# A decoder of four layers on one core: cross attention's inputs loaded by the stage ahead, a self attention with its norm and a longer lead, experts with three buffers

## The reference, cut to what matters

```python
def sublayer(x):              # layer norm without a weight, residual
    return x + f((x - mean(x)) / sqrt(var(x) + 1e-5))
# layer 0: self attention (16 heads of 64, weights of 1024 columns), mixing with the context, coupled twist
# layer 1: gated recurrence, cross attention (16 heads of 8), experts (32, 6 chosen)
# layer 2: linear attention, cross attention, experts (8, 2 chosen)
# layer 3: rotary attention (two), cross attention, experts (32, 2 chosen, at most 70 tokens each) with 16 shared adapters
```

## Time and profile before

| | us |
|---|---|
| median of 3 runs | 4221.11 (4218.85 to 4239.77) |
| the profiled execution | 4235.5 |
| its span | 4233.7 |
| PE busy | 3635.9 (86%) |
| DVE busy | 2555.3 (60%) |
| ACT busy | 2097.0 (50%) |
| POOL busy | 1549.6 (37%) |
| the 16 DMA engines, mean | 110 GB/s |

### The profile page before, as it was taken

One profiled execution on the slowest core, in us unless ns is written; L12 is line 12 of the kernel. 1 busy time (PEld: TensorE's weight loads), 2 busy tenths in 40 slices (PEclk: granted clock), 3 DMA queues, 4 the chain that ended last, 5 costly groups with the idle time before them and its releaser, 6 DMA issues. The chain is left out here.

```text
span 4233.7 us, 113113 instructions
## 1 busy us (share of the span) xinstructions
PE 3635.9 (86%) x48174; PEld 2505.2 (59%) x48174; DVE 2555.3 (60%) x4447; ACT 2097.0 (50%) x2832; POOL 1549.6 (37%) x1827
## 2 busy tenths in 40 slices
PE   7976459999997888799999988988899999972798
PEld 5654237777775446477777764434477777751565
DVE  4522568877774445578777753346688777746443
ACT  3344437666664232267666652344476666650010
POOL 1100037667661000267667620013466766610000
PEclk9998779999998899899999998989999999985897
DMA  4062045655651430456655621100465566510674
GB/s 147 2 253 102 2 108 148 151 145 148 157 140 37 98 85 3 96 137 152 152 142 150 157 50 55 54 8 9 105 150 147 141 156 150 143 42 0 159 184 123
DMA packets 203247, 464.39 MB, mean 110 GB/s; under 512 B 87486, under 2 KB 94398, under 8 KB 202590
## 3 DMA queue, kind: packets, MB, share of 16 engines
q1 hardware_dynamic: 200622, 455.30, 41.3%
q10 hardware_dynamic: 2160, 2.29, 0.2%
HBM read 212.72 MB, written 1.72 MB: 51 GB/s over the span
## 5 line engine op out<-in xcount | busy, mean ns | idle before, releaser
L1435 DVE TENSOR_REDUCE x_bank_top<-ps 112x1 f32<-112x500 f32 x2304 | 1418.7, 671 | 472.0 <-PE ps L1151 465.6
L1287 ACT ACTIVATE x_probs_t<-ps 128x1344 f32<-128x1344 f32 x768 | 991.2, 1291 | 215.0 <-PE ps L1168 210.4
L1168 PEld LDWEIGHTS ps<-x_queries,x_keys 128*128 128x128 bf16 x9216 | 488.7, 98 | 333.5 <-issue 152.9
L1151 PE MATMUL ps<-x_keys,x_queries 96*112 96x500 bf16 x2304 | 633.7, 381 | 25.0 <-DMA x_keys<-x_key_part 15.6
L1168 PE MATMUL ps<-x_queries,x_keys 128*128 128x112 bf16 x9216 | 585.4, 213 | 41.2 <-ACT x_probs_t L1287 36.6
L1181 PE MATMUL ps<-x_probs_t,x_values 128*32 128x112 f32 x18432 | 492.2, 263 | 5.3 <-ACT x_probs_t L1287 4.1
L1181 PEld LDWEIGHTS ps<-x_probs_t,x_values 128*32 128x32 f32 x18432 | 445.0, 111 | 70.1 <-issue 65.2
L1368 POOL TENSOR_TENSOR x_key_part<-x_key_whole,x_nothing 128x500 bf16<-128x500 f32 x270 | 336.8, 1247 | 259.3 <-ACT x_key_whole L1272 259.3
L1372 POOL TENSOR_TENSOR x_key_part<-x_key_left,x_nothing 128x500 bf16<-128x500 f32 x270 | 340.3, 1260 | 21.2
L1139 PE MATMUL ps<-x_wv,x_ctx_t 128*128 128x128 f32 (+1 forms) x2304 | 329.9, 287 | 9.8 <-issue 9.8
L1151 PEld LDWEIGHTS ps<-x_keys,x_queries 96*112 96x112 bf16 x2304 | 258.9, 131 | 127.9 <-DVE x_bank_top L1435 35.9
(11 more groups left out here) (455 smaller groups left out, 4526.8 us busy)
## 6 DMA issues: line engine op xcount, KB each, us to landing
x_keys<-x_key_part SPq DMA_DIRECT2D x1143, 192.0 KB, 3.7
x_ctx_t<-in_ctx_t SPq DMA_DIRECT2D x96, 750.0 KB, 6.1
cm_ctx_n<-in_ctx_n SPq DMA_DIRECT2D x32, 768.0 KB, 6.5
cm_ctx_t<-in_ctx_t SPq DMA_DIRECT2D x32, 750.0 KB, 8.7
e_share<-m_weight_scratch SPq DMA_DIRECT2D x32, 490.0 KB
e_spread_out<-m_slot_scratch SPq DMA_DIRECT2D x32, 490.0 KB
x_queries<-x_query_part SPq DMA_DIRECT2D x558, 28.0 KB, 2.7
e_share<-m_weight_rows SPq DMA_DIRECT2D x32, 448.0 KB, 5.8
```

Source lines behind the costliest of these rows:

```text
L1151: nc.tensor.matmul(ps[0:RW, n, 0:KB], queries[i // 2 % 2][0:TALL, p, i % 2, :], keys[i % 2][0:TALL, p, KB * n:KB * n + KB], start=True, st ...
L1168: mm = nc.tensor.matmul(ps[:, TURNED + c // VC, RW * (c % VC):RW * (c % VC) + RW], keys[i % 2][:, p, KT * c:KT * c + KT], queries[i // 2 % ...
L1287: nc.scalar.activation(probs_t[PROBS[p]].rearrange("k (n c) r -> k n (c r)", c=VC), ps[:, TURNED:TURNED + VR, 0:VC * RW], ACT.Exp, scale=s ...
L1435: nc.vector.tensor_reduce(bank_top[0:RW, p, n:n + 1], ps[0:RW, n, 0:KB], AX_X, ALU.max).then_inc(topped, 1)
```

## The change

Four things are changed.

1. `CrossLead` allocates the weights, constants, first three contexts and `keys` buffers of a cross attention ahead of the stage before it, and that stage (gated recurrence, linear attention, the second rotary attention) issues their loads behind its own. The cross attention issues none of them. In its start PE does `lead_keys` 0 and 1 ahead of the four `power` steps; SP issues all six `key_slots` of the first half, then three `query_slots` of each half, and ACT the other three `query_slots` of each half.
2. `self_attention_0` has the norm inside its block, its loads at the block's start with three semaphores in place of one, scores two pairs ahead, two `mix` buffers, and another order on PE, ACT and DVE.
3. `experts_by_slot` has three buffers in place of two, its loops written out, `share` and `spread_out` issued ahead of the weights, and a gather of three bfloat16 parts of the tokens against bfloat16 marks.
4. `mixture_3` makes those parts: three copies on ACT and two subtractions on POOL.

```diff
 def self_attention_0(chip):
+            for c in range(CH):
+                norm.centre(pe, c)
+            for c in range(CH):
+                norm.power(pe, c)
+            pe.wait_ge(qk_landed, 4 * 16)
...
-            for n in range(-1, NP_):
+            for n in range(-2, NP_):
                 if n >= 0:
                     turn(n)
-                if n + 1 < NP_:
-                    make_scores(n + 1)
-                if n > 0 and n % 2 == 0:
-                    project_out(n // 2 - 1)
                 for g, t in halves(n):
                     project(g, t)
                 if n >= 0:
                     mix_values(n)
-                if n + 1 < NP_:
+                if n + 2 < NP_:
+                    make_scores(n + 2)
+                if 0 <= n + 1 < NP_:
                     make_values(n + 1)
+                if n > 0 and n % 2 == 0:
+                    project_out(n // 2 - 1)
...
         def _(act):
                 if n >= 0:
                     keep_turned(n)
                 for g, t in halves(n):
                     if t % 4 < 2:
                         keep_made(g, t)
-                if n + 1 < NP_:
-                    exponentials(n + 1)
+                if 0 <= n + 1 < NP_:
                     keep_values(n + 1)
+                if n + 2 < NP_:
+                    exponentials(n + 2)
...
+class CrossLead:
+    def load(self, sp):
+        weight(self.wk, "Wk", self.wk_landed)
...
+        for i in range(CONTEXTS):
+            source = dram["ctx_t"][bass.ds(i, 1)].rearrange("a p n -> (a p) n")
+            sp.dma_start(self.ctx_t[i][:], source).then_inc(self.ctx_landed[i], 16)
+        rows = dram["pair_rows"].rearrange("r (p n) -> r p n", p=PR)
+        for u in range(2):
+            sp.dma_start(self.keys[u][TALL:P].bitcast(F32), rows).then_inc(self.rows_landed, 16)
...
 def cross_attention(chip, layer, scale):
             sp.wait_ge(zeros_ready, 2 * PARTS)
+            sp.wait_ge(lead_low, NB_)
+            for s in range(SLOTS):
+                key_slots(sp, 0, 0, s)
             sp.wait_ge(q_low, 2)
-            for s in range(SLOTS // 2):
-                query_slots(sp, 0, 0, s)
-            sp.wait_ge(lead_low, NB_)
-            for s in range(SLOTS // 2):
-                key_slots(sp, 0, 0, s)
-            for s in range(SLOTS // 2):
-                query_slots(sp, 0, 1, s)
+            for h in range(2):
+                for s in range(SLOTS // 2):
+                    query_slots(sp, 0, h, s)
...
             for c in range(CH):
                 norm.centre(pe, c)
-            norm.power(pe, 0)
-            norm.power(pe, 1)
             pe.wait_ge(wk_landed, 2 * 16)
             lead_keys(0)
-            norm.power(pe, 2)
-            norm.power(pe, 3)
             lead_keys(1)
+            for c in range(CH):
+                norm.power(pe, c)
             lead_keys(2)
...
 def experts_by_slot(chip, weight_rows, slot_rows, slot_of, token_parts, CAP):
-    PAIRS, SUBS, LOADS = 16, 2, 6
+    PAIRS, SUBS, LOADS, DEEP = 16, 2, 6, 3
+            for n in range(PAIRS):
+                u = n % DEEP
+                if n >= DEEP:
+                    sp.wait_ge(used[u], n // DEEP)
...
                 for t in range(NP_):
-                    mm = nc.tensor.matmul(ps[:, gather_bank(u), 0:2 * CAP], by_token[:, t, :], marks[u][:, t].rearrange("p e k -> p (e k)"),
-                                          start=(t == 0), stop=(t == NP_ - 1))
+                    for k in range(PARTS):
+                        mm = nc.tensor.matmul(ps[:, gather_bank(n), 0:2 * CAP], token_parts[k][:, t, :], marks[n % 2][:, t].rearrange("p e k -> p (e k)"),
+                                              start=(t == 0 and k == 0), stop=(t == NP_ - 1 and k == PARTS - 1))
...
+        @block.gpsimd
+        def _(pool):
+            pool.wait_ge(s["stats_ready"], 1)
+            pool.wait_ge(s["tokens_kept"], 2)
+            for k in range(1, PARTS):
+                pool.wait_ge(s["part_kept"], k)
+                whole = tokens if k == 1 else token_rests[k - 2]
+                nc.gpsimd.tensor_tensor(token_rests[k - 1][:], whole[:], token_parts[k - 1][:], ALU.subtract).then_inc(s["part_rest"], 1)
```

More of the change, by code:

```diff
@@ L324, in project @@
                 if t % 4 == 1:
-                    wait(pe, added, g - 2 + t // 4)
+                    wait(pe, added, g - 2)
+                if t == 0 and g % 2 == 0:
+                    norm.wait_scaled(pe, max(g // 2, 1))
                 w = (wq, wk)[t // 4]
@@ L433, in keep_values @@
                 nc.scalar.copy(v[n % 2][:], ps[:, VALUES:VALUES + 2, :]).then_inc(v_kept, 1)
-            act.wait_ge(landed, 8 * 16)
+            nc.scalar.preload_act_table_set("natural_log")
+            for c in range(CH):
+                norm.square(act, c)
+            for c in range(CH):
+                norm.log(act, c)
+            for c in range(CH):
+                norm.inverse(act, c)
+            act.wait_ge(qk_landed, 4 * 16)
             for t in range(TILES):
@@ L494, in add @@
                                                ALU.add, ALU.add).then_inc(added, 1)
+            for c in range(CH):
+                norm.scale(dve, c)
+            for c in range(CH):
+                norm.wait_scaled(dve, c)
             nc.vector.memset(ps[:, SCORES:SCORES + 2, :], 0.0).then_inc(banks_clear, 1)
-            dve.wait_ge(landed, 8 * 16)
+            dve.wait_ge(qk_landed, 4 * 16)
             for t in range(TILES):
@@ L500, in _ @@
                     keep_made(0, t)
+            dve.wait_ge(out_landed, 3 * 16)
             dve.wait_ge(bias_done, 1)
             nc.vector.tensor_tensor(bo_sum[:], ps[:, VALUES, 0:1], bo[:], ALU.add).then_inc(bias_ready, 1)
-            for n in range(-1, NP_):
-                if n + 1 < NP_:
-                    shift(n + 1)
-                if n > 0 and n % 2 == 0:
-                    add(n // 2 - 1)
+            for n in range(-2, NP_):
                 for g, t in halves(n):
@@ L510, in _ @@
                         keep_made(g, t)
-                if n + 1 < NP_:
-                    add_up(n + 1)
                 if n >= 0:
                     keep_mix(n)
+                if n + 2 < NP_:
+                    shift(n + 2)
+                    add_up(n + 2)
+                if n > 0 and n % 2 == 0:
+                    add(n // 2 - 1)
             add(GROUPS - 1)
+    chip.release()
 def context_mixing(chip):
@@ L1010, in cross_attention @@
         nothing = sbuf("nothing", [P, KB])
-        keys = [sbuf("keys%d" % u, [P, PR, WIDE], BF16) for u in range(2)]
         queries = [sbuf("queries%d" % u, [P, PR, 2, RW], BF16) for u in range(2)]
@@ L1036, in _ @@
         def _(sp):
-            def load(dst, name, landed):
-                sp.dma_start(dst, chip.dram[name]).then_inc(landed, 16)
-            def weight(name):
-                return "L%d_xattn_%s" % (layer, name)
             def context(i):
@@ L1867, in one_step @@
                 mm.then_inc(up_done, 1)
-                if more:
-                    gather(i + (u + 1) // 2, (u + 1) % 2)
+                if n + 1 < PAIRS:
+                    gather(n + 1)
                 pe.wait_ge(hidden_ready, n + 1)
@@ L1887, in _ @@
                 nc.tensor.matmul(ps[:, c, 0:CT], zero[:], chunk[c], start=True, stop=False, skip_group_check=True)
-            gather(0, 0)
-            all_steps(pe, one_step)
+            gather(0)
+            for n in range(PAIRS):
+                one_step(n)
             for c in range(CH):
@@ L1970, in mixture_3 @@
         by_token, square = sbuf("by_token", [P, NP_, P]), sbuf("square", [P, NP_, P])
+        tokens, token_rests = sbuf("tokens", [P, NP_, P]), [sbuf("token_rest%d" % k, [P, NP_, P]) for k in range(2)]
         stats = sbuf("stats", [P, NP_, NS])
@@ L2154, in _ @@
                 sp.dma_start(dst[:], chip.dram[name]).then_inc(s[landed], 16)
+            chip.lead.load(sp)
         @block.tensor
@@ L2378, in _ @@
             sp.dma_start(w[:], chip.dram["L3_attn_%sweights" % tag]).then_inc(s["landed"], 16)
+            if last:
+                chip.lead.load(sp)
         @block.tensor
@@ L2752, in decoder @@
             for stage in (self_attention_0, context_mixing):
-                normalise(chip, chip.x, chip.xn, True)
+                if stage not in NORMALISING:
+                    normalise(chip, chip.x, chip.xn, True)
                 stage(chip)
                 chip.end_stage()
-        for stage in STAGES:
-            if stage not in NORMALISING:
-                normalise(chip, chip.x, chip.xn, True)
-            stage(chip)
-            chip.end_stage()
+        with ExitStack() as rest:
+            for stage in STAGES:
+                if stage in LED:
+                    chip.lead = CrossLead(chip, LED[stage], rest)
+                if stage not in NORMALISING:
+                    normalise(chip, chip.x, chip.xn, True)
+                stage(chip)
+                chip.end_stage()
+                if stage in CROSS:
```

(1 more changed line is left out.)

205 lines of the change are left out of this document (108 added, 97 removed).

## The result

The change makes the kernel faster, by less than was forecast: a median of 4183.8 us (four executions, 4168.8 to 4190.7) against 4225.5 for the kernel before, a ratio of 0.9903, interval 0.9876 to 0.9929. That is 42 us less, where 66 were forecast and a time of 4155. One execution of the kernel before, in a later group, took 8339.4 us, twice the usual, and is left out of every figure here. The profiled execution took 4190.68 us, span 4188.9, against 4235.5 and 4233.7.

The account below looks back on a forecast made before the run. PE was taken to bound the kernel, waiting for loads in the last experts. Savings of 53 (experts), 8 (self attention) and 5 us (cross attentions) sum to 66, giving 4155 us against the median 4221.1; range 4138 to 4182.

Parts of the forecast that it names:

- The experts' three buffers: Last experts: loads get two steps, some 27 us, to land, so PE's wait and the slow clock behind it go.
- The gather: Experts: 48 bfloat16 matmuls take 2.85 us where the gather took 3.81, saving 0.95 us in each of 15 steps.
- the last step: Experts: the last of sixteen steps takes 12.1 us, its sum 6.25; 6 us less saved if at the low clock.
- The experts become bound by DMA: Rival, experts: loads of 15.5 us that do not overlap make 248, saving 21 instead of 53; 4187 us, chance 0.07.
- come at 14.4 us each: Experts, a case inside the forecast: loads arriving every 14.4 us would make the saving 15 us less.
- The start: Self attention: loads issued at the block's start let PE begin 9.8 us earlier, the first tile near 22.8 to 22.9.
- Sum 22.0: nothing gained: Self attention, steady state: two pairs still take 22.0 us, with 1.1 us idle in another place.
- my chain through ACT: Self attention: ACT's fixed order makes a pair without `project_out` take 9.9 us, where PE's own work is 8.76.
- scores two ahead pay: Rival, self attention: tile 2 finds its bank free, 12 us gained, time 4143; self attention better had chance 0.05.
- Cross attentions and the preload: Three cross attentions: loads issued in the stages ahead bring the first score 1.7 us earlier in each, 5 in all.
- Code: Rival, experts: written-out loops wait for about 11 instruction fetches, 12 us each, 132 us in all; 4287 us, chance 0.03.
- The parts of the gather: Last stage's preparation: three copies and two subtractions are hidden behind idle ACT and cost nothing; without that cover 15 us.

Follow-up runs that it names:

- r_after: The changed kernel itself, unaltered, run again in five rounds: seven executions, 4158.4 to 4210.6 us, ratio 0.9914; the profiled one took 4158.4 us.
- q_deep2: The changed kernel with two places instead of three in each ring of the experts, float32 slot rows kept: 4182.1 us, ratio 0.9913.
- r_low: The changed kernel with the experts' slot rows stored and spread as bfloat16, three places kept: median 4153.7 us, ratio 0.9863.
- e10_light_both: The changed kernel with a step's last matmuls over one of four chunks and products over their first 448 columns, all loads kept: 4152.7 us.

## Why the prediction was wrong

**The step that failed** is in "The experts' three buffers": "the DMA engines were 0.89 busy and moved 238 GB/s for 12 us, which is the 2.9 MB of a step. PE needs more than 12. So the wait goes". The term that was too small is the time that a step's loads take: 12 us, where the first profile has 15.9 and the quicker one 14.2. The 12 us were read from a queue that had just filled and held one step's loads. With three places it never empties, and under way each packet takes longer than it did at the start. Per step and busy DMA engine there are 20 packets of 7168 B (five rows of each of four spread loads, as the run with 80 rows bears out), 16 of 3072 and 8 of 1536. With their mean durations in us, over the packets that start in the stretch named:

| kernel | stretch | DMA share | 7168 B | 3072 B | 1536 B | us a step |
|---|---|---|---|---|---|---|
| before, as read for the forecast | 3949.5 to 3961.5 | 0.89 | 0.463 | 0.147 | 0.066 | 12.1 |
| before | 4050 to 4110 | 0.74 | 0.482 | 0.146 | 0.065 | 12.5 |
| changed, first profile | 3913 to 3930 | 0.94 | 0.471 | 0.172 | 0.078 | 12.8 |
| changed, first profile | 4050 to 4110 | 0.94 | 0.555 | 0.236 | 0.134 | 15.9 |
| changed, `r_after` | 4050 to 4110 | 0.94 | 0.491 | 0.217 | 0.110 | 14.2 |
| changed, two places (`q_deep2`) | 4050 to 4110 | 0.77 | 0.455 | 0.158 | 0.072 | 12.2 |
| bfloat16 slots (`r_low`) | 4050 to 4110 | 0.69 | 0.426 | 0.157 | 0.070 | 9.7 |

(The last row has ten of its 20 spread packets at 0.236, half as long in bytes.) The third row has a full queue too, and its packets are still short; in the fifth, those of 7168 B are hardly longer. So a full queue goes with longer packets only after a while and not by one fixed amount, and why they grow was not shown. 15.9 is about the step that the first profile settles at. 14.2 is more than TensorE's 13.31 as well, but so little that the steps loaded ahead cover it for ten steps.

**The gather, the step, the last step.** 2.93 us (2.85 forecast) and 13.31 (13.4) were right. The last step takes 12.13 us, as forecast (12.1), its sum at full speed (compare):

```profile
4170.38 6.25 PE L1921 MATMUL ps<-e_spread_out,e_result 70*128 70x448 f32 x16 [0.55 <-ACT e_result L1946]
```

In five of the seventeen profiles of this study that have the change that sum ran at the low clock after all and the last step took 19.2 to 19.4 us. The first step takes 17.4, not 15.9. Of the 22.8 us that the sixteen steps of the first profile save (268.7 became 245.9), 9.0 are thus the last step's; the fourteen between the first and the last went from 16.46 to 15.45 each, and 0.88 of that 1.01 is what the gather is shorter. So in this execution the third place brought next to nothing by itself, as `q_deep2` with 15.15 us a step bears out. At the quick rate it did pay: steps of 13.31 us in a row, where the two profiles with two places and float32 slots have 15.15 and 15.29 on average. The rule of the Trainium skill, page "TensorE: Matmul & The Clock Gate", section "Back-to-back issue gap", some 81 ns for each pair of weight load and matmul, would have made the gather 3.9 us, an estimate; the trace has 61 ns at 140 columns and doesn't agree.

**The rivals.** "The experts become bound by DMA", 15.5 us a step and 4187, given 0.07, is what the first profile shows, at 15.6 a step and 246 us for the sixteen (the rival has 248). The bounds of the forecast's own sum hold loads that "come at 14.4 us each", "15 less", which is near the quicker rate; over the executions in the three profiles of the changed kernel the last stage's saving is 24, 51 and 52 us. The mechanism was thus seen and given too little weight. "Against: the second step's loads flowed in 12 us" was the same reading a second time, so it was no evidence against.

**Self attention.** The start was right to 0.3 us, and the tile's wait for ACT's bank is there, but shorter: 1.01 and 0.28 us, 8.5 in all where POOL had cost 12.2. "Sum 22.0: nothing gained" failed: two pairs take 20.8 to 22.1. The pair with `project_out` takes 12.4 or 12.5 us and once 13.1 (forecast 12.1), the one without 8.4 to 9.7, where my chain through ACT gave 9.9; that chain was too long by up to 1.5 us, and the pair comes out at about PE's own work (8.76 by the forecast's addition). The last pairs, which were to "come out as now", are shorter too: the last two distances between turnings were 8.56 and 10.23 us and are 6.04 and 10.79, in `r_after` 6.04 and 9.14. The rival "scores two ahead pay" (12 us) is the nearer one with 9 to 10, and the start gives 5 to 6 rather than 8.

**Cross attentions and the preload.** 5 forecast, some 8 measured, and the stages ahead don't grow. The first score came only 0.4 us earlier in the first cross attention, not 1.7: it now waits for its queries, half of whose issues stand on SP behind six key issues that took 4.73 us, not 3.7. But over the three it came 0.4, 2.6 and 1.4 us earlier, 4.4 in all, so the forecast's 5 was about right for what it counted. Up to the 25th of the 768 score matmuls of each the gain is 7.8 us. So the early loads bring some 3 us more within the next 20 us, which the forecast left out.

**Code.** The written-out loops fetch ten packets of instructions more, 375 against 365, where the rival counted 11. It was wrong on their price: in the experts PE has no idle time without a releaser.

```profile
q8 instruction: 375, 6.14, 0.6%
```

**The parts of the gather** are hidden, as forecast: the copy behind them still finds ACT idle for 45.75 us.

```profile
3908.23 0.59 ACT L2092 COPY m_slot_of<-ps 128x512 f32<-128x512 f32 x1 [45.75 <-PE ps L2065]
```

**Whole.** The three medians of the changed kernel lie 42, 48 and 48 us under those of before, each on its chip. The terms for an execution at the quick rate are 51 + 15 + 8 = 74 and more than the forecast 66, at the low rate 24 + 15 + 8 = 47; they are differences to the profiled execution of before (4235.5), and 4158.4 of `r_after` is 77 under it, 4190.7 of the first profile 45. What was wrong was to count on the quick rate alone.

## What to carry to other kernels

A rate read from a queue that had just filled was an upper bound here. Before a deeper ring is priced, multiply the packets on the busiest DMA engine by their duration in a stretch where the queue has been full for some time. If that comes near the engine's own step or above it (here 14.2 and 15.9 us against 13.31), cut bytes first. Here half a megabyte less (exact integers in bfloat16) did what the third place did not, and made the third place needless. A stage that runs that close to its loads also took a different time from one execution to the next: 423.2 us in one profile of the changed kernel, 395.3 in another, so that one profile can mislead by 28 us.

## What the hardware showed that was not expected

- Two kernels move 192 to 195 GB/s in the same stretch, one with its DMA engines busy for 0.94 of the time, one for 0.71. So here the share went with the duration of the packets and not with the bytes moved: packets of 3072 B took 0.236 us in the one with the queue always full and 0.157 to 0.166 in those with bfloat16 slots, those of 7168 B 0.555 and 0.42 to 0.43 (4050 to 4110).
- The same loads went at 192 to 209 GB/s in one execution and at 215 to 235 in another, with the rate falling during the stage in both, and in `e10_light_both` too. Neither another source row nor a second queue brought the quick rate; the reads and products of the spread rows are not the whole cause of the fall. What sets the rate stays open. The Trainium skill's page "DMA: Bandwidth & Descriptors", section "Bandwidth", notes that with both cores of a memory domain streaming each gets roughly half of its bandwidth; whether the neighbour core was at work in these executions, no run here shows.
- 70 rows seem as dear as 80 on the DMA engines (223 to 229 GB/s with 80, against 215 to 220 in the changed kernel's profile of the same group, with medians 0.2 us apart).
- Rotary attention took 243.8 us once, 14 more than its usual, in a kernel whose code for it was the same; no cause was sought.
